# Second attention scores of a graph kernel: the one-hots of sources and destinations on two engines

## The reference

```python
feat = (h @ fc_w.T).reshape(n, heads, out_feats)
el = jnp.sum(feat * attn_l, axis=-1)
er = jnp.sum(feat * attn_r, axis=-1)
e = jax.nn.leaky_relu(el[src] + er[dst], 0.2)
...
rst = jax.ops.segment_sum(feat[src] * a[..., None], dst, num_segments=n)
```

## Time and profile before

| | us |
|---|---|
| median of 3 runs | 2163.2 |
| lowest and highest | 2162.46, 2171.91 |
| the profiled execution, its own time | 2164.12 |
| its span, first to last instruction | 2162.0 |

### The profile page before, as it was taken

The page is one execution under the profiler, slowest core; times in us unless marked ns, Lnnn a source line. Parts: engine busy times, 40 slices in busy tenths (PEclk is TensorE's granted clock), DMA queues, the critical chain, the costliest instruction groups (busy, mean ns, idle before and its releaser), DMA issues.

```text
span 2162.0 us, 28858 instructions
## 1 busy us (share of the span) xinstructions
PE 1510.2 (70%) x7701; PEld 1142.3 (53%) x7702; DVE 1450.5 (67%) x2290; ACT 419.2 (19%) x780; POOL 1365.3 (63%) x1396
## 2 busy tenths in 40 slices
PE   6346656656558443788666687877787787579997
PEld 4235545545446343676555444655555555368874
DVE  3357777777776787676444366677677666777766
ACT  1100000000004000100000033444444444110127
POOL 0477777777720888777777723677777777135544
PEclk9657877877779555899787889888877777689999
DMA  3654444444414665444444336999999999778821
GB/s 97 164 133 124 126 125 123 126 126 122 121 36 129 173 171 146 135 130 129 115 120 119 110 108 214 316 338 342 340 341 342 344 331 345 284 254 294 292 70 60
DMA packets 234908, 406.13 MB, mean 188 GB/s; under 512 B 33199, under 2 KB 171621, under 8 KB 228197
## 3 DMA queue, kind: packets, MB, share of 16 engines
q0 software_dynamic: 73216, 219.89, 32.9%
q1 hardware_dynamic: 161637, 185.66, 27.3%
HBM read 330.93 MB, written 74.48 MB: 188 GB/s over the span
## 4 chain that ended last, share of the span: by engine, by line
POOL 48%; PE 19%; issue 18%; DMA 6%; DVE 6%; SPq 1%; ACT 1%; DVEq 0%; ACTq 0%; POOLq 0%
POOL row_space L875 44%; PE ps L1189 9%; DMA row_space<-tab_kv,src_i 3%; PE ps L1290 3%; DMA item_v<-row_space 2%; PE ps L1399 2%; POOL base L884 2%; POOL acc L884 1%; PE ps L1419 1%; POOL arena L884 1%; PE ps L990 1%; PE ps L962 1%; PE ps L1085 1%; DMA arena<-rows_block_dst 0%; PE ps L1214 0%
## 5 line engine op out<-in xcount | busy, mean ns | idle before, releaser
L875 POOL DMA_INDIRECT row_space<-tab_feat,src_i x760 | 752.1, 990 | 300.8 <-issue 231.2
L875 POOL DMA_INDIRECT row_space<-tab_kv,src_i x416 | 393.3, 946 | 195.6 <-issue 124.3
L1189 PE MATMUL ps<-arena 128*128 128x257 f32 (+1 forms) x1664 | 420.4, 414 | 121.2 <-DVE arena L2157 114.8
L1189 PEld LDWEIGHTS ps<-arena 128*128 128x128 f32 x1664 | 338.3, 207 | 196.6 <-issue 138.7
L1290 PE MATMUL ps<-arena 128*128 128x265 f32 x768 | 241.2, 480 | 110.6 <-DVE ps L2400 47.3
L1085 PE MATMUL ps<-acc,arena 128*128 x832 | 289.3, 508 | 0.0
L2151 DVE TENSOR_TENSOR arena<-row_space,ps 128x1280 f32<-128x1280 f32 (+1 forms) x94 | 174.3, 1854 | 142.0 <-DMA row_space<-tab_feat,src_i 140.2
L1290 PEld LDWEIGHTS ps<-arena 128*128 128x128 f32 x768 | 181.2, 242 | 159.0 <-issue 117.6
L1569 ACT COPY acc<-ps 128x265 f32<-128x265 f32 (+2 forms) x75 | 28.2, 376 | 1114.7 <-PE ps L1189 542.8
L1085 PEld LDWEIGHTS ps<-acc,arena 128*128 128x128 f32 x832 | 198.0, 250 | 39.0
L1969 DVE TENSOR_TENSOR arena<-row_space,ps 128x1024 f32<-128x1024 f32 x104 | 126.8, 1219 | 134.6 <-PE ps L1085 84.8
(11 more groups left out here) (380 smaller groups left out, 2190.9 us busy)
## 6 DMA issues: line engine op xcount, KB each, us to landing
item_v<-row_space SPq DMA_DIRECT2D x52, 1024.0 KB, 8.0
row_space<-item_v SPq DMA_DIRECT2D x52, 1024.0 KB, 5.0
arena<-rows_block_dst SPq DMA_DIRECT2D x104, 128.0 KB
row_space<-tab_feat,src_i POOLq DMA_INDIRECT x760, 2.8
scores<-rows_block_dst SPq DMA_DIRECT2D x52, 128.0 KB
arena<-rows_src_low SPq DMA_DIRECT2D x52, 128.0 KB
row_space<-tab_kv,src_i POOLq DMA_INDIRECT x416
arena<-rows_type SPq DMA_DIRECT2D x52, 128.0 KB
```

Of the source, the lines that this page charges most:

```text
L875: nc.gpsimd.indirect_dma_start(rows_of_slot(s)[:, g, :], None, table, bass.IndirectOffsetOnAxis(ap=src_i[:, item:item + 1], axis=0),).then ...
L1189: last = nc.tensor.matmul(ps[:, SUM_BANKS:2 * SUM_BANKS][:, bass.ds(bs[g], 1), 0:width].rearrange("p a d -> p (a d)"), onehot[:, s % 2, g, ...
```

## The change

- The destinations' one-hot moves to ScalarE, as two activations over 1024 elements: the square of the byte row minus the partition number, and relu of one minus that, in place. They have a semaphore of their own, `dst_onehot_made`, and TensorE waits for it too. The squares of group n+1 are issued ahead of the relu of group n, and the squares wait for `score_mm`, which TensorE raises when the products of the group before in that place are made.
- VectorE compares the source row alone (1024 elements), with a column in PSUM that is broadcast, in place of a scalar in SBUF. The row of block numbers for `hi_onehot` lies in PSUM as well. Four small copies put them there.
- `bcast` gets four places, and SyncE loads all four ahead.

```diff
 SHARE_BANK, IOTA_AT = 3, 256
+NUMBERS_AT = 480
...
-        bcast = v[0][:, 0:GROUP * P].bitcast(U8).rearrange("p (s a e) -> p s a e", s=2, a=2)
+        bcast = v[0].bitcast(U8).rearrange("p (s a e) -> p s a e", s=SLOTS, a=2)
...
-        bcast_in = [sem(f"item_rows_broadcast{s}") for s in range(2)]
+        bcast_in = [sem(f"item_rows_broadcast{s}") for s in range(SLOTS)]
+        dst_onehot_made = [sem(f"destination_onehot_made{s}") for s in range(2)]
...
+                def spread_both(u, s, first):
+
+                    for k, made in ((0, onehot_made), (1, dst_onehot_made)):
+                        if not first and k == 0:
+                            sp.wait_ge(made[s % 2], nth(u, s) + HALF)
+                        if not first and k == 1:
+                            sp.wait_ge(made[s % 2], nth(u, s) - 1)
+                        row = flat[k][bass.ds(u * (STEP * P // 2) + s * GROUP * P // 2, GROUP * P // 2)]
+                        sp.dma_start(bcast_words[:, s, k], row.partition_broadcast(P)).then_inc(bcast_in[s], 16)
+
                 if keep is None:
-                    with nc.sync.Fori(0, TURNS) as u:
+                    for s in range(SLOTS):
+                        spread_both(0, s, True)
+                    with nc.sync.Fori(0, TURNS - 1) as u:
                         for s in range(SLOTS):
-                            spread(u, s)
+                            spread_both(u + 1, s, False)
...
                         pe.wait_ge(onehot_made[s % 2], nth(u, s) + (layer * HALF + 2))
+                        pe.wait_ge(dst_onehot_made[s % 2], nth(u, s) + 1)
...
-            idle("score2")
+
+            begin(act, "score2", ["dve", "pe"])
+
+            def dst_squares(u, s):
+
+                z = s % 2
+                act.wait_ge(bcast_in[s], u * 32 + (32 + (broadcasts(1) if s < 2 else 0)))
+                act.wait_ge(score_mm[z], nth(u, s) + HALF)
+                nc.scalar.activation(onehot_t[:, z, 1], bcast[:, s, 1], ACT.Square,
+                                     bias=minus_part_no[:]).then_inc(act_step, 1)
+                step.add()
+
+            def dst_relu(s, still):
+
+                act.wait_ge(act_step, step.value() - still)
+                nc.scalar.activation(onehot_t[:, s % 2, 1], onehot_t[:, s % 2, 1], ACT.Relu, scale=-1.0,
+                                     bias=ones[:, 0:1]).then_inc(dst_onehot_made[s % 2], 1)
+
+            dst_squares(0, 0)
+            with nc.scalar.Fori(0, TURNS - 1) as u:
+                step.enter(u, SLOTS)
+                for s in range(SLOTS):
+                    dst_squares(u + (s + 1) // SLOTS, (s + 1) % SLOTS)
+                    dst_relu(s, 1)
+                step.leave(TURNS - 1)
...
             def onehots(layer, u, s):
 
                 z = s % 2
-                dve.wait_ge(bcast_in[z], nth(u, s) * 32 + (32 + broadcasts(layer)))
-                vec.tensor_scalar(onehot_t[:, z], bcast[:, z], part_no[:], None,
+                dve.wait_ge(bcast_in[s], u * 32 + (32 + (broadcasts(layer) if s < 2 else 0)))
+                own = ps[:, 4 * z:4 * z + 1, NUMBERS_AT + BLOCKS:NUMBERS_AT + BLOCKS + 1].rearrange("p a x -> p (a x)")
+                vec.tensor_tensor(onehot_t[:, z, 0], bcast[:, s, 0], own.broadcast_to([P, GROUP * P]),
                                   ALU.is_equal).then_inc(onehot_made[z], 1)
...
                 def hot(u, s):
 
+                    at = 4 * ((s + 1) % 2)
                     then(vec.tensor_tensor(
                         hi_onehot[:, s % 2, :, 0:BLOCKS],
-                        iota_free[:, 0:BLOCKS].unsqueeze(1).broadcast_to([P, GROUP, BLOCKS]),
+                        ps[:, at:at + 1, NUMBERS_AT:NUMBERS_AT + BLOCKS].broadcast_to([P, GROUP, BLOCKS]),
```

More of the change, by code:

```diff
@@ L258, in graph_layers @@
         v = views(2 * GROUP * P, 2 * GROUP * P, 2 * GROUP * 32, 2 * GROUP * PICKS * H2)
-        bcast = v[0][:, 0:GROUP * P].bitcast(U8).rearrange("p (s a e) -> p s a e", s=2, a=2)
-        bcast_words = v[0][:, 0:GROUP * P].bitcast(I16).rearrange("p (s a e) -> p s a e", s=2, a=2)
+        bcast = v[0].bitcast(U8).rearrange("p (s a e) -> p s a e", s=SLOTS, a=2)
+        bcast_words = v[0].bitcast(I16).rearrange("p (s a e) -> p s a e", s=SLOTS, a=2)
         onehot_t = v[1].bitcast(BF16).rearrange("p (s a e) -> p s a e", s=2, a=2)
@@ L500, in broadcasts @@
         def broadcasts(layer):
-            return 16 * HALF + 32 * HALF * (layer - 1) if layer else 0
+            return 16 * HALF + 32 * TURNS * (layer - 1) if layer else 0
         @block.sync
@@ L1596, in _ @@
             end()
-            idle("score2")
+            begin(act, "score2", ["dve", "pe"])
[17 more added lines that the diff above has]
+                step.leave(TURNS - 1)
+            for s in range(SLOTS):
+                if s + 1 < SLOTS:
+                    dst_squares(TURNS - 1, s + 1)
+                dst_relu(s, 1 if s + 1 < SLOTS else 0)
+            for z in range(2):
+                act.wait_ge(dst_onehot_made[z], HALF)
+            end()
             soft(0, "soft2", H2, ITEMS // 4)
@@ L1874, in gat_scores @@
                 w = BLOCKS * heads
+                for z in range(2):
+                    then(vec.tensor_copy(ps[:, 4 * z, NUMBERS_AT:NUMBERS_AT + BLOCKS], iota_free[:, 0:BLOCKS]))
+                    then(vec.tensor_copy(ps[:, 4 * z, NUMBERS_AT + BLOCKS:NUMBERS_AT + BLOCKS + 1], part_no[:]))
                 el_v, er_v = er[:, :, 0:heads], er[:, :, heads:2 * heads]
@@ L1879, in gat_scores, with first_onehots @@
                 signal(parts_made)
[L1880 to L1887, removed]
+                def first_onehots():
+                    if own_onehots:
+                        onehots(layer, 0, 0)
+                        hot(0, 0)
+                        onehots(layer, 0, 1)
+                    else:
+                        dve.wait_ge(bcast_in[0], 32)
+                        hot(0, 0)
+                    did(vec.memset(hi_onehot[:, :, :, BLOCKS:PICKS], 1.0))
                 def hot(u, s):
+                    at = 4 * ((s + 1) % 2)
                     then(vec.tensor_tensor(
                         hi_onehot[:, s % 2, :, 0:BLOCKS],
-                        iota_free[:, 0:BLOCKS].unsqueeze(1).broadcast_to([P, GROUP, BLOCKS]),
+                        ps[:, at:at + 1, NUMBERS_AT:NUMBERS_AT + BLOCKS].broadcast_to([P, GROUP, BLOCKS]),
                         src_hi[:, bass.ds(u * STEP + s * GROUP, GROUP)].unsqueeze(2).broadcast_to([P, GROUP, BLOCKS]),
@@ L1917, in turn @@
                             onehots(layer, u + (s + 2) // SLOTS, (s + 2) % SLOTS)
-                hot(0, 0)
+                first_onehots()
                 all_but(0)
```

## The result

| | before | after |
|---|---|---|
| median, us | 2162.8 (4 runs) | 2207.4 (4 runs) |
| the profiled execution, its span | 2162.0 | 2205.3 |
| ratio to before, 95% interval | | 1.0193 [1.0171, 1.0215] |

What follows compares the result with a forecast made beforehand. No engine was full; the chain of waits ran over GpSimd for 48% of the span. score2's +49.8 us less 3.3 of reserve gave +46.5, so 2210 us, 2.1% slower, range 2194 to 2227.

Steps and rivals of the forecast that it cites:

- The ring: In score2, squares(n+1), relu(n), products(n), squares(n+2) wait in a closed circle: 3.69 us a group in place of 2.70.
- The length of score2: score2's last product ends at 897.1 instead of 847.27, 49.8 us longer; soft2 and sum2's start move with it.
- The wait for the slot: GpSimd, its 136 gathers out by 872.3, waits some 87 us until group 6's slot is free at 959.3.
- the count of places: GpSimd has places for 17 groups, 136 gathers; the gather of group 17 needs the slot of group 6.
- The 3.3 us: Before group 17, GpSimd can be at most 3.3 us earlier unless sum2 starts earlier; sum2 delay beyond that delays the end.
- The sum: End of the kernel: +49.8 for score2 less 3.3 of reserve gives +46.5 us.
- the tail: Part behind the last gather: everything there was to move by the same amount, with nothing added.
- The upper bound: With register steps, 0.2 more in hand-overs and 2 us for first loads: ring 3.95, end +62 us, 2225.
- The gathers alone decide: Rival: GpSimd's gathers, undisturbed beside score2, end 40 us earlier, 2124 us; chance 0.02.
- The ring is not closed: Rival: the slower of VectorE and ScalarE sets score2's pace, 2.2 us a group; end 27 us earlier, 2137; chance 0.05.

Runs made afterwards that it cites:

- Experiment 1: Changed kernel with ScalarE's two activations swapped, relu of group n before squares of group n+1; 2149.3 us, ratio 0.9913 to the kernel before.
- experiment 5: Relu first, with VectorE's two comparisons on SBUF operands again as before the change, source row alone; ratio 0.9895 to the kernel before.
- relu first: The kernel of Experiment 1, relu of group n issued ahead of squares of group n+1; timed again at 2148.9 us, ratio 0.9906.
- Experiment 6: Relu first, with VectorE making both one-hots of every fourth group in one 2048-element SBUF comparison; 2141.9 us, ratio 0.9871 to the kernel before.
- Experiment 3: Changed kernel with 48 spare additions on GpSimd, one ahead of each of the first 48 gathers; ratio 1.0187, against 1.0193 without.
- experiment 4: Kernel before with 48 spare additions on GpSimd, one ahead of each of the first 48 gathers; ratio 1.0150.
- experiment 2: Kernel before with four places for the byte rows and nothing else of the change; ratio 1.0019.

## Why the prediction was right

- **The ring.** It was forecast at 3.69 us a group and measured at 3.56. The hand-overs are 0.10 and not 0.14 and 0.12, and the products 1.18 to 1.23. ScalarE waits for TensorE 65.7 us, forecast 75. Experiment 1 shows that the ring is the cause: one link is taken out by order alone, and the kernel goes from 1.9% slower to 0.9% faster.
- **The length of score2.** Forecast +49.8 us. The last product ends at 889.35 + 0.18 = 889.53, 42.3 us later than 847.27. The 0.13 us a round over 50 rounds are 6.5 of the difference, and the first rows landed 1.3 us earlier.
- **GpSimd.** The wait for the slot was forecast at 87 us, 872 to 959, and is 80.8, 871.8 to 952.6; the 6 us are those of the ring. The gathers run at 1.25 us beside score2 ((870.85 - 702.02) / 135), and the gain from that was nothing, as the count of places had it. The Trainium skill (GPSIMD Engine Reference, Key points) says that GpSimd contends for its SBUF interfaces with VectorE's instructions in a two-port mode or with two SBUF inputs. The traces agree: experiment 5 puts the two comparisons with SBUF operands back, and a gather takes 1.34 us again where relu first has 1.26. No trace shows the port mode itself. The prediction named both comparisons, L1868 and L1891, as culprits. Experiment 6 points to the first: with the block one-hot left in PSUM, 13 one-hots of 2048 elements cost 11.2 us, 0.86 each, and in the kernel before both kinds together cost 0.78 a group (40.6 / 52). Experiment 3 shows the wait to be idle reserve.
- **The 3.3 us.** GpSimd had no reserve before (no time in which it only waits for a slot): experiment 4 lets a delay through whole, and experiment 2 shows that an earlier sum2 gave it nothing. The change traded a GpSimd without reserve for one with 81 us of it, at the price of a later sum2.
- **The sum.** +46.5 forecast, +44.5 measured in the medians and +43.3 in the spans. Of the latter 40.0 are the restart's, where 46.5 were forecast, and 3.3 the tail's, which the prediction put at nothing. So the agreement is better than the terms, by luck: the ring was sized 6.5 us too long and the tail made up half of it. By the ratio, 1.9% of 2162.8, the change costs some 42 us.
- **The upper bound.** Its terms were added wrongly. A ring of 3.69 with 0.1 on each of two activations and 0.2 in hand-overs is 4.09 us and not 3.95, and the end by it (46.5 + 50 x 0.4 + 2 us above 2163) is 2232 and not 2225. The round measured, 3.56, lies well inside either.
- **The rivals.** "The gathers alone decide" fell with the wait of 80.8 us. "The ring is not closed" is what experiment 1 builds; its price had been put at 27 us below before, 2137, and came out at 0.9%, 19 us. It missed TensorE's start of a turn, and ScalarE's 2.24 us where relu needs its own squares; 2.2 was taken. The last product there ends at 829.6, 18 us before 847.3 where 24 were reckoned.

## What to carry to other kernels

When work moves to an idle engine, write down for each buffer who waits for whom in issue order, and look for a circle: two instructions in the wrong order on one engine can put its work and another engine's in series though each has room. Before counting a gain, find the place where the freed engine next stops (here a count of 136 gathers) and how late it arrives there; that number bounds the gain. A cover that was worth nothing in one version, like the four places, can be worth 1.5% in the next, so parts of a change are judged together with the one that follows them.

## What was not expected of the hardware

- VectorE's comparisons with SBUF operands slow GpSimd's gathers out of proportion to their time. From the first to the last of the 136 gathers, less 135 x 1.25 us, the loss is 40.6 us with 52 comparisons of 1.30 us (kernel before), 44.3 with 52 of 1.28 (experiment 2), 12.5 with 52 of 0.76 us (experiment 5), 12.3 with 13 of 1.28 us among 39 with a PSUM operand (experiment 6), and 1.1 with the PSUM operand throughout (experiment 1). Halving the comparison cut the loss to less than a third. The block one-hot has SBUF operands in the first three of these; its part was not tried alone.
- TensorE's 2.1 to 2.2 us at each turn of its loop, some 1.8 of them for loading block numbers, hidden until the pace came near 2.2 us a group.
- The part behind the last gather, whose instructions are the same in all these kernels, takes 900.2 to 907.2 us in the traces of this case. Single profiles can't settle a difference of a few microseconds in the whole.
